# The last head group's chain set out anew, the first tile's turning and up products ahead of the last value products, three chunks' weights among the expert tiles

## Chip, core and metric

One core of one Trainium2 chip runs the whole program. The metric is the device time of one execution in microseconds (us).

## The reference

One transformer block over 2048 tokens of 128 channels, float32:

```
mod = silu(c) @ wmod                      # shift, scale and gate for two halves
h   = layernorm(x) * (1 + ca) + sa
x   = x + ga * (softmax(q k^T / sqrt(8) + alibi, causal) v @ W_proj + b_proj)   # 16 heads of 8
h   = layernorm(x) * (1 + cb) + sb
p   = softmax(h @ router_w^T)             # 8 experts, the best two per token
w   = softmax(of the two best p)
x   = x + gb * sum over the two of w * scale[e] * (silu(h @ w1[e]^T) @ w2[e]^T)
```

The experts are 512 wide. A token's two experts depend on the data.

## The kernel before, in words

**Attention.** The 16 heads go in four groups of four. Tokens are in four chunks of 512 columns. A first pass finds row maxima (scores on TensorE, maxima on VectorE, which the profile calls DVE), a second makes scores anew, exponentials on ScalarE (ACT; `probs`, L1295) and value products on TensorE (L744). A group has 36 steps of the second pass (`STEPS`); each step has two half-steps of two heads, and `step(p)` (L787) issues scores of step p, then the value products of step p-1. Step 36 (`NSTEP`) has the last value products alone. Chunk 3 begins at step 21. On every engine the order is written out by hand: tables at the top (L148 to L185) say at which step, or at which expert tile, an operation is issued.

**The last group's chain.** In the fourth group the first pass is through early, and the steps carry the second half of the block for chunks 0 to 2: `project(c)` on TensorE (`PROJECT`, L157, half of it behind each half-step), `residual(c)` with the statistics on DVE (L1032), `deviation(c)` on GpSimd (POOL; L1340, at step `DEVIATION_AT` and, for chunk 2, behind the group), `scale_tokens(c)` on DVE (L911; it normalises four tiles of 128 tokens into `slots`), `turn_late(c)` on TensorE (L650, `TURN`), `features(c, 1)` on ScalarE (L1215), `logits(c)` on TensorE (L656, `LOGITS`), `keep_logits` and `route(c, 0..5)` on DVE (L1041, L1046), two small exponentials on ScalarE (`route_exp`, L1252, `ROUTE_EXP`: step and position among the step's exps), `count(k)` on TensorE (L666, `COUNT`) and `place(k, 0..2)` on DVE (L1090). Part 5 of `route` makes the two weights of a token; only the join at the end reads them. POOL meanwhile also scales earlier values by their sums (`scale_values`, L1421, two multiplies or adds of 128x512; chunk 2 at step 20, chunk 3 at step 21).

**The experts.** Tokens are sorted by expert in three parts: part 0 is chunk 0, part 1 chunks 1 and 2, part 2 chunk 3. `send_part(k)` (L1451) has POOL write each token row twice into `slot_scratch` by an indirect DMA of 128 rows, with a memset (`pause`) ahead of each: 8 sends for part 0, 16 for part 1, 8 for part 2. Within part 1, `SEND_BREAK` says after how many sends POOL makes the deviation of chunk 3. There are 53 tiles of 128 rows: 15, 23 and 15. The SP queue loads a tile (L562; a part's first load waits for all of its sends) and stores results (L567). For tile j TensorE turns the rows (`turn_tile`, L837, one tile ahead), ScalarE makes features (L1316), TensorE the up products (`up`, L844), ScalarE silu (L1322), TensorE the down products of the tile before (`down`, L861). DVE copies each tile's first weights into a ring of four (`stage`, L1131, three tiles ahead) and multiplies the result by the gate (`keep`, L1143). Chunk 3's own chain runs among the tiles by `LATE_PROJECT` and the other LATE tables (L179 to L182). `gather_part(k)` (L1462) has POOL fetch each token's two results when all tiles of the part are stored; `join` (L1151) on DVE adds them with the weights.

**Between the two.** Behind step 36 TensorE waits for chunk 2's features, its logits and part 0's places, turns tiles 0 and 1 and starts the up products. ScalarE copies the last values (`copy_values`, L1262) and then makes tile 0's features. DVE, in its list at L1157, makes the weights of chunks 0 to 2 behind the placing of part 1, then scales by the sums of chunk 3 (`scale_sums`, `add_sums`, L970) and enters the tile loop, where it stages tile 3 first.

## Time and profile before

| | |
|---|---|
| median of three runs | 585.2 us (584.65 to 585.96) |
| the profiled execution | 584.42 us, of which the span between first and last instruction is 582.6 |
| TensorE, matmul (PE) and weight load (PEld) | 495.7 us (85%) and 266.1 (46%) |
| DVE | 456.4 us (78%) |
| ScalarE (ACT) | 403.3 us (69%) |
| POOL | 176.2 us (30%) |
| mean granted TensorE clock | 0.955 |

The page cuts the span into 40 slices of 14.6 us; each digit is a busy share in tenths, and PEclk the clock that TensorE was granted, in tenths of its full 2.4 GHz.

```profile
PE   4756777889999999999999998998988997999960
DVE  3689999989989998988998998986688744653442
ACT  4922456669878888888888888787788464555520
POOL 3410000010022120410214001057075681870884
PEclk9975899999999999999999999999899997999995
```

Setup takes the first four slices, attention goes on to about 448 us, the expert tiles to about 563, and the last slice is POOL's last gathers and the joins. All times in texts and rows are microseconds from the start of the span.

### The profile page before, as it was taken

How to read it: one execution, taken by the hardware profiler on the slowest of the kernel's cores; microseconds unless marked ns; L12 is line 12 of the kernel's file. 1: busy time of each engine (PE TensorE's matmuls, PEld its weight loads, DVE VectorE, ACT ScalarE, POOL GpSimd, SP SyncE). 2: the span in 40 equal slices, each digit the busy share in tenths (PEclk: the TensorE clock that was granted, in tenths of full speed). 3: DMA queues.
4: the chain of work that ended last, by engine and by line, in shares of the span. 5: the costliest groups of instructions: out<-in, count | busy, mean ns of one | idle time of the engine just before them, and what ended most of it. 6: DMA issues, size and time to landing. Idle time of an engine off the chain costs nothing.

```text
span 582.6 us, 15494 instructions
## 1 busy us (share of the span) xinstructions
PE 495.7 (85%) x5876; PEld 266.1 (46%) x5876; DVE 456.4 (78%) x775; ACT 403.3 (69%) x778; POOL 176.2 (30%) x291
## 2 busy tenths in 40 slices
PE   4756777889999999999999998998988997999960
PEld 2422233343243343243343333334434987999960
DVE  3689999989989998988998998986688744653442
ACT  4922456669878888888888888787788464555520
POOL 3410000010022120410214001057075681870884
PEclk9975899999999999999999999999899997999995
DMA  6593121000012530222300000100221212333332
GB/s 156 198 292 74 30 56 29 1 3 4 11 29 60 169 131 2 92 74 44 78 10 4 2 2 4 30 9 6 88 78 57 78 60 75 104 102 92 106 87 72
DMA packets 38263, 37.86 MB, mean 65 GB/s; under 512 B 7088, under 2 KB 33904, under 8 KB 37560
## 3 DMA queue, kind: packets, MB, share of 16 engines
q1 hardware_dynamic: 35808, 32.26, 20.0%
q0 software_dynamic: 2048, 4.20, 2.4%
q8 instruction: 49, 0.80, 0.6%
q10 hardware_dynamic: 336, 0.42, 0.2%
q14 instruction: 22, 0.18, 0.1%
HBM read 20.05 MB, written 16.61 MB: 63 GB/s over the span
## 4 chain that ended last, share of the span: by engine, by line
PE 51%; ACT 8%; POOL 8%; DVE 6%; issue 4%; DMA 1%; ACTq 0%; POOLq 0%; DVEq 0%
PE pv L744 18%; PE b L777 13%; ACT probs L1295 6%; PE b L716 6%; PE b L851 4%; PE b L868 4%; POOL raw L1470 4%; DVE part L1012 3%; PE b L691 3%; POOL pause L1442 2%; POOL slot_scratch L1449 1%; ACT raw L1265 1%; PE b L646 1%; PE b L842 1%; PE b L663 1%
## 5 line engine op out<-in xcount | busy, mean ns | idle before, releaser
L1295 ACT ACTIVATE probs<-b 128x512 f32<-128x512 f32 (+1 forms) x576 | 298.6, 571 | 77.2 <-PE b L691 34.3
L1012 DVE TENSOR_REDUCE part<-b 128x2 f32<-128x1024 f32 (+2 forms) x320 | 327.4, 1060 | 25.2 <-PE b L691 11.7
L744 PE MATMUL pv<-probs,v_cur 128*32 128x256 f32 (+1 forms) x2432 | 175.3, 370 | 0.3 <-ACT probs L1295 0.2
L777 PE MATMUL b<-aug 55*128 55x512 bf16 (+3 forms) x640 | 113.2, 352 | 24.8 <-ACT probs L1295 20.6
L716 PE MATMUL b<-aug 52*128 52x512 bf16 (+3 forms) x640 | 115.8, 361 | 20.1 <-DVE part L1012 17.2
L777 PEld LDWEIGHTS b<-aug 55*128 55x128 bf16 x640 | 36.9, 93 | 135.7 <-ACT probs L1295 129.8
L744 PEld LDWEIGHTS pv<-probs,v_cur 128*32 128x32 f32 x2432 | 49.9, 108 | 66.5 <-issue 38.9
L851 PE MATMUL b<-hTt,inverse 128*128 128x128 f32 x424 | 58.1, 281 | 1.3 <-ACT hTt L1316 1.1
L868 PE MATMUL b<-w2T_sb,hst 128*128 x424 | 57.1, 279 | 1.2 <-ACT hst L1322 0.8
L851 PEld LDWEIGHTS b<-hTt,inverse 128*128 128x128 f32 x424 | 53.2, 197 | 1.9 <-issue 1.3
L868 PEld LDWEIGHTS b<-w2T_sb,hst 128*128 128x128 f32 x424 | 52.5, 195 | 1.8 <-issue 1.6
L716 PEld LDWEIGHTS b<-aug 52*128 52x128 bf16 x640 | 33.5, 94 | 36.3 <-DVE part L1012 29.0
L1322 ACT ACTIVATE hst<-b 128x512 f32<-128x512 f32 x53 | 31.6, 597 | 23.0 <-PE b L851 21.6
L1141 DVE COPY inverse<-aug 128x512 f32 x53 | 26.2, 496 | 22.8 <-issue 19.7
L1413 POOL CAST nmp<-nmax 128x16 bf16<-128x16 f32 x16 | 3.4, 211 | 131.5 <-POOLq L191 131.3
L1442 POOL MEMSET pause<- 128x512 f32 x56 | 31.8, 567 | 33.7 <-DMA y_scratch<-aug 27.2
L1316 ACT ACTIVATE hTt<-b,modc 128x128 f32<-128x128 f32 x53 | 24.1, 456 | 25.6 <-PE b L842 16.3
L1149 DVE TENSOR_TENSOR aug<-b,gate 128x128 f32<-128x128 f32 x53 | 15.3, 290 | 30.7 <-issue 19.2
L1449 POOL DMA_INDIRECT slot_scratch<-slots,spots x32 | 32.8, 1024 | 8.9 <-POOL pause L1442 8.9
L1470 POOL DMA_INDIRECT raw<-y_scratch,spots x32 | 31.8, 993 | 9.0 <-POOL pause L1442 6.5
L691 PE MATMUL b<-maskQ,identh 64*128 64x128 bf16 (+1 forms) x512 | 32.4, 209 | 0.0
L691 PEld LDWEIGHTS b<-maskQ,identh 64*128 64x128 bf16 x512 | 25.6, 98 | 12.3 <-issue 1.8
(150 smaller groups left out, 379.0 us busy)
## 6 DMA issues: line engine op xcount, KB each, us to landing
xt<-slot_scratch SPq DMA_DIRECT2D x53, 64.0 KB, 1.9
y_scratch<-aug SPq DMA_DIRECT2D x53, 64.0 KB
slot_scratch<-slots SPq DMA_DIRECT2D x3, 1024.0 KB, 8.6
aug<-q_scratch SPq DMA_DIRECT2D x6, 384.0 KB
aug<-k_scratch SPq DMA_DIRECT2D x6, 384.0 KB
w2T_sb<-in_w2T SPq DMA_DIRECT2D x1, 2048.0 KB, 7.6
aug<-in_w1T SPq DMA_DIRECT2D x8, 256.0 KB
q_scratch<-pieces SPq DMA_DIRECT2D x4, 384.0 KB, 2.8
```

Of the source, the lines that this page charges most:

```text
L691: ins = mm(pair[half][:, at_ + c0:at_ + c1], identh[k, h, :], table[k, h, c0:c1], start=False, stop=True, skip_group_check=True)
L716: ins = mm(pair[half][:, at_:at_ + w], q_aug[buf][n, b, t:t + P], k_aug[buf][n, b, c * CW:c * CW + w], start=True, stop=True)
L744: return mm(pv[32 * hh:32 * hh + 32, c0:c1], v_cur[:, kb, hh, :], probs[:, step_ % 2, hh, at_:at_ + c1 - c0], start=(kb == 0 and c0 == 0), ...
L777: done.append(mm(pair[half][:, at_:at_ + w], k_aug[g % 2][n, b, kb * P:kb * P + P], q_aug[g % 2][n, b, (j + 1) * CW - w:(j + 1) * CW], sta ...
L851: last = mm(b1[:, j % 2, f * P:(f + 1) * P], w1s[:, k, f * P:(f + 1) * P], hTt[:, j % 2, :], start=True, stop=True)
L868: last = mm(b1[:, 2 + j % 2, 0:C], hst[:, j % 2, f, :], w2T[:, ds(e * FC + f, 1), :], start=(f == 0), stop=(f == FC - 1))
L1012: ins = nc.vector.tensor_reduce(dst, b1[:, slot:slot + 2, at_:at_ + w], AX.X, ALU.max)
L1295: nc.scalar.activation(probs[:, p % 2, hh, 0:w], b2[:, (n2 - 1) % RING2, 0:w], ACT.Exp).then_inc(exp_done, 1)
L1322: nc.scalar.activation(hst[:, j % 2, :, :].rearrange("p f t -> p (f t)"), b1[:, j % 2, :], ACT.Silu).then_inc(silu_s, 1)
L1442: own.inc(nc.gpsimd.memset(pause[:, :], 0.0))
L1449: nc.gpsimd.indirect_dma_start(slot_dram, bass.IndirectOffsetOnAxis(ap=spots[:, b, n:n + 1], axis=0), slots[:, n, :], None).then_inc(sent_ ...
L1470: nc.gpsimd.indirect_dma_start(yfin[:, n, b, :], None, y_dram[0:BASE[k + 1] * P, :], bass.IndirectOffsetOnAxis(ap=spots[:, b, n:n + 1], ax ...
```

## The change

The chain of chunks 1 and 2 in the last group is moved one to three steps forward; the tile tables of chunk 3 move two tiles back; the break in part 1's sends moves from 8 sends to 12. DVE scales chunk 2's tokens before the last piece of part 0's placing. TensorE turns tile 0 (into another bank, `turned_rows`) and makes its up products before the last value products. ScalarE makes tile 0's features and silu and tile 1's features before it copies the last values. The weights of chunks 0 to 2 go to tiles 22, 24 and 26. `turn_tile` and `up` are moved up in the file unchanged but for the bank.

```diff
 STACK_AT = {True: [START[1], START[1] + 2, START[1] + 4, START[1] + 6], False: [0, 5, 7, 11]}
 LAST_OUT, LAST_IN, LAST_INVERT, LAST_BACK, LAST_INVERSE = [5, 11], [6, 12], [INVERT, 14], [9, 15], [10, 16]
 LAST_SCALE = {13: 0, 18: 1}
-DEVIATION_AT = {19: 0, 22: 1}
-PROJECT = {16: 0, 19: 1, 24: 2}
-TURN = {19: 0, 22: 1, 28: 2}
-LOGITS = {21: 0, 23: 1, 29: 2}
-ROUTE_EXP = {(22, 4): (0, 0), (24, 4): (1, 0), (27, 4): (0, 1), (30, 2): (2, 0), (31, 4): (1, 1), (35, 4): (2, 1)}
-COUNT = {25: 0, 33: 1}
+DEVIATION_AT = {19: 0, 20: 1}
+PROJECT = {16: 0, 18: 1, 24: 2}
+TURN = {19: 0, 20: 1, 27: 2}
+LOGITS = {21: 0, 22: 1, 28: 2}
+ROUTE_EXP = {(21, 4): (0, 0), (24, 2): (1, 0), (26, 2): (0, 1), (29, 2): (2, 0), (30, 4): (1, 1), (34, 2): (2, 1)}
+COUNT = {25: 0, 32: 1}
 
 
 PARTS = [(0, TPC), (TPC, 3 * TPC), (3 * TPC, NT)]
@@ -176,13 +176,14 @@
 STORE_BEHIND = 6
 
 
-LATE_PROJECT, LATE_RESIDUAL, LATE_TOKENS, LATE_TURN, LATE_LOGITS, LATE_KEEP = 3, 4, 6, 7, 9, 10
-LATE_ROUTE = {10: 0, 12: 1, 13: 2, 14: 3, 15: 4, 21: 5}
-LATE_EXP = {11: 0, 16: 1}
-LATE_COUNT, LATE_PLACE = 16, {17: 0, 18: 1, 19: 2}
+LATE_PROJECT, LATE_RESIDUAL, LATE_TOKENS, LATE_TURN, LATE_LOGITS, LATE_KEEP = 3, 4, 8, 9, 11, 12
+LATE_ROUTE = {12: 0, 14: 1, 15: 2, 16: 3, 17: 4, 23: 5}
+LATE_EXP = {13: 0, 18: 1}
+LATE_COUNT, LATE_PLACE = 18, {19: 0, 20: 1, 21: 2}
+WEIGHTS_AT = {22: 0, 24: 1, 26: 2}
 JOIN_AT = {27: 0, 28: 1, 29: 2, 30: 3, 44: 4, 46: 5, 48: 6, 50: 7, 52: 8}
 STORE_AT = {36: 0}
-SEND_BREAK = 8
+SEND_BREAK = 12
 
 
 def take(e, s, n):
@@ -425,6 +426,10 @@
 
             return raw[:, g % 2, j * CW:(j + 1) * CW]
 
+
+        def turned_rows(j):
+
+            return b2[:, j % 2, 0:P] if j else b1[:, 1, 0:P]
 
         def last_part(q):
 
@@ -676,6 +681,23 @@
                               start=False, stop=(i == n_b - 1), skip_group_check=True)
                 last.then_inc(count_ps, 1)
 
+            def turn_tile(j):
+                k = j % ROWS_DEEP
+                pe.wait_ge(xt_in[k], 16 * (j // ROWS_DEEP + 1))
+                if j >= 2:
+                    pe.wait_ge(tT_s, j - 1)
+                nc.tensor.transpose(turned_rows(j), xt[:, k, :], ident[:, :]).then_inc(tT_ps, 1)
+
+            def up(j):
+                k = j % DEEP
+                pe.wait_ge(w1s_s, j + 1)
+                pe.wait_ge(tT_s, j + 1)
+                if j >= 2:
+                    pe.wait_ge(silu_s, j - 1)
+                for f in range(FC):
+                    last = mm(b1[:, j % 2, f * P:(f + 1) * P], w1s[:, k, f * P:(f + 1) * P], hTt[:, j % 2, :], start=True, stop=True)
+                last.then_inc(up_ps, 1)
+
             freed = []
             n_exp = [0]
 
@@ -820,6 +842,9 @@
                         if p in COUNT:
                             count(COUNT[p])
                     if last and p == NSTEP:
+                        pe.wait_ge(hT_s, 2 * NC_ - 1)
+                        turn_tile(0)
+                        up(0)
                         for b in range(PAIRS):
                             value_products(p, b)
 
@@ -833,23 +858,6 @@
             group(2, False, False)
             group(3, False, True)
 
-
-            def turn_tile(j):
-                k = j % ROWS_DEEP
-                pe.wait_ge(xt_in[k], 16 * (j // ROWS_DEEP + 1))
-                if j >= 2:
-                    pe.wait_ge(tT_s, j - 1)
-                nc.tensor.transpose(b2[:, j % 2, 0:P], xt[:, k, :], ident[:, :]).then_inc(tT_ps, 1)
-
-            def up(j):
-                k = j % DEEP
-                pe.wait_ge(w1s_s, j + 1)
-                pe.wait_ge(tT_s, j + 1)
-                if j >= 2:
-                    pe.wait_ge(silu_s, j - 1)
-                for f in range(FC):
-                    last = mm(b1[:, j % 2, f * P:(f + 1) * P], w1s[:, k, f * P:(f + 1) * P], hTt[:, j % 2, :], start=True, stop=True)
-                last.then_inc(up_ps, 1)
 
             def owner_of(j):
 
@@ -868,15 +876,12 @@
                     last = mm(b1[:, 2 + j % 2, 0:C], hst[:, j % 2, f, :], w2T[:, ds(e * FC + f, 1), :], start=(f == 0), stop=(f == FC - 1))
                 last.then_inc(down_ps, 1)
 
-            pe.wait_ge(hT_s, 2 * NC_ - 1)
             pe.wait_ge(lraw_s, NC_ - 1)
-            pe.wait_ge(place_s, 1)
-            turn_tile(0)
             for j in range(TILES):
                 if j + 1 < TILES:
                     turn_tile(j + 1)
-                up(j)
                 if j:
+                    up(j)
                     down(j - 1, owner_)
                 owner_ = owner_of(j)
                 if j == LATE_PROJECT:
@@ -1167,8 +1172,10 @@
             for k in range(1, 5):
                 route(0, k)
             residual(2)
-            place_part(0)
+            place(0, 0)
+            place(0, 1)
             scale_tokens(2)
+            place(0, 2)
             for k in range(1, 5):
                 route(1, k)
             keep_logits(2)
@@ -1178,8 +1185,6 @@
             for k in range(1, 5):
                 route(2, k)
             place_part(1)
-            for c in range(3):
-                route(c, 5)
             scale_sums(NC_ - 1)
             add_sums(NC_ - 1)
             for j in range(TILES):
@@ -1197,6 +1202,8 @@
                     route(NC_ - 1, LATE_ROUTE[j])
                 if j in LATE_PLACE:
                     place(NPART - 1, LATE_PLACE[j])
+                if j in WEIGHTS_AT:
+                    route(WEIGHTS_AT[j], 5)
                 if j in JOIN_AT:
                     join(JOIN_AT[j])
             keep(TILES - 1)
@@ -1300,8 +1307,6 @@
                         features(TURN[p], 1)
                     if last and (p, HG) in ROUTE_EXP:
                         route_exp(*ROUTE_EXP[p, HG])
-                if last:
-                    copy_values(g, NC_ - 1)
                 return n2
 
             n2 = group(0, True, False, 0)
@@ -1313,7 +1318,7 @@
                 act.wait_ge(tT_ps, j + 1)
                 if j >= 2:
                     act.wait_ge(up_ps, j - 1)
-                nc.scalar.activation(hTt[:, j % 2, :], b2[:, j % 2, 0:P], ACT.Identity, bias=modc[:, 2:3], scale=modc[:, 3:4]).then_inc(tT_s, 1)
+                nc.scalar.activation(hTt[:, j % 2, :], turned_rows(j), ACT.Identity, bias=modc[:, 2:3], scale=modc[:, 3:4]).then_inc(tT_s, 1)
 
             def silu(j):
                 act.wait_ge(up_ps, j + 1)
@@ -1322,7 +1327,10 @@
                 nc.scalar.activation(hst[:, j % 2, :, :].rearrange("p f t -> p (f t)"), b1[:, j % 2, :], ACT.Silu).then_inc(silu_s, 1)
 
             tile_features(0)
-            for j in range(TILES):
+            silu(0)
+            tile_features(1)
+            copy_values(G - 1, NC_ - 1)
+            for j in range(1, TILES):
                 if j + 1 < TILES:
                     tile_features(j + 1)
                 silu(j)
```

## Rows read from the trace of the kernel before

**Rows 1.** The chain that ended last, two steps: start us, us, engine, line.

```profile
535.69 1.60 DMA y_scratch<-aug
...
576.12 2.48 DMA raw<-y_scratch,spots
```

**Rows 2.** Timeline of POOL, 446 to 481: start us, us, engine, line, op.

```profile
446.09 0.52 POOL L1442 MEMSET pause<- 128x512 f32 x1 [4.87 <-DVE spots L1116]
...
463.55 0.23 POOL L1345 TENSOR_SCALAR rstd<-mv 128x4 f32<-128x4 f32 x1 [2.72 <-DVE mv L908]
...
465.14 0.65 POOL L1442 MEMSET pause<- 128x512 f32 x1
...
479.71 0.97 POOL L1449 DMA_INDIRECT slot_scratch<-slots,spots  x1 [0.28 <-POOL pause L1442]
```

**Rows 3.** Timeline of TensorE in the tiles, 455 to 491.

```profile
455.47 1.16 PE L851 MATMUL b<-hTt,inverse 128*128 128x128 f32 x8 [0.28 <-DVE inverse L1141]
...
458.36 1.06 PE L851 MATMUL b<-hTt,inverse 128*128 128x128 f32 x8
...
464.05 1.06 PE L851 MATMUL b<-hTt,inverse 128*128 128x128 f32 x8
...
467.16 1.06 PE L851 MATMUL b<-hTt,inverse 128*128 128x128 f32 x8
...
471.80 1.06 PE L851 MATMUL b<-hTt,inverse 128*128 128x128 f32 x8
...
479.33 1.15 PE L868 MATMUL b<-w2T_sb,hst 128*128 x8 [0.79 <-ACT hst L1322]
...
483.74 0.48 PE L842 MATMUL b<-ident_sb,xt 128*128 128x128 f32 x1 [3.25 <-DMA xt<-slot_scratch]
...
490.33 1.06 PE L851 MATMUL b<-hTt,inverse 128*128 128x128 f32 x8
```

**Rows 4.** Three stretches: busy us by engine (x count), granted clock, DMA, GB/s.

```profile
410.00:415.00 5.00, 4.75 (x38) 1.63 (x34) 2.82 (x5) 3.85 (x9) 0.00 (x0) 0.66 0.34 105
...
480.00:492.00 12.00, 8.75 (x55) 8.56 (x54) 4.27 (x13) 3.16 (x7) 0.68 (x1) 0.72 0.26 72
...
498.00:510.00 12.00, 12.00 (x110) 12.00 (x110) 8.60 (x32) 6.50 (x13) 10.07 (x15) 1.00 0.37 106
```

**Rows 5.** Timelines of POOL, DVE and TensorE, steps 18 to 21.

```profile
398.35 1.27 POOL L1427 TENSOR_TENSOR raw<-raw,inverse 128x512 f32<-128x512 f32 x1
...
398.41 2.63 DVE L917 TENSOR_SCALAR slots<-x_sb,mv,rstd 128x128 f32<-128x128 f32 x2 [1.48 <-POOL rstd L1354]
...
403.81 0.69 DVE L1037 TENSOR_TENSOR x_sb<-b,x_sb 128x512 f32<-128x512 f32 x1 [0.19 <-PE b L646]
...
406.51 0.39 PE L777 MATMUL b<-aug 55*128 55x512 bf16 x2
...
407.30 1.11 DVE L917 TENSOR_SCALAR slots<-x_sb,mv,rstd 128x128 f32<-128x128 f32 x4 [1.48 <-POOL rstd L1354]
```

**Rows 6.** Timelines of ScalarE and DVE where attention ends, 446 to 452.

```profile
446.70 0.66 ACT L1295 ACTIVATE probs<-b 128x256 f32<-128x256 f32 x2 [0.28 <-PE b L691]
...
449.71 1.28 ACT L1322 ACT_TABLE_LOAD   x1
...
451.00 0.60 ACT L1322 ACTIVATE hst<-b 128x512 f32<-128x512 f32 x1
...
451.10 0.70 DVE L974 STREAM_TRANSPOSE q<-raw 128x512 f32<-128x512 f32 x1
```

**Rows 7.** Timelines of TensorE, the SP queue and DVE, 439 to 449.

```profile
439.07 0.64 PE L744 MATMUL pv<-probs,v_cur 128*32 128x256 f32 x8
...
442.21 0.20 PE L672 MATMUL b<-both,lowerb 128*128 128x64 bf16 x1
...
442.51 6.24 SPq L562 DMA_DIRECT2D xt<-slot_scratch  x7
...
445.85 0.16 DVE L1082 TENSOR_SCALAR psm<-wtop 128x4 f32<-128x4 f32 x1
```

## The prediction

> **What bounds the kernel now.** I read the chain of waits from its end first. It leaves TensorE for the last time with the store of tile 37 at 535.69, and from there POOL's row gathers hold it until the last lands at 578.6 [rows 1]. Those gathers start when tile 37 is stored and their number doesn't change, so the time at which TensorE is through tile 37 sets the end: a microsecond won by tile 16 is won at the end, if nothing between waits anew.
>
> What TensorE waits for before tile 37 is part 1. On POOL, its first send follows the placing at 446.09, eight sends take until 460.83, then POOL stands 2.72 us for the variances of chunk 3, spends 1.59 on the deviation, and the other eight end at 480.68 [rows 2]. On TensorE, tile 14 turns tile 15's rows first; that turning waits 3.25 us, until 483.74 [rows 3]. The windows show the second price: the granted clock averages 0.72 from 480 to 492, which at the two levels of 1.2 and 2.4 GHz is 6.7 us at the lower one [rows 4]. From 483.74 to the up products of tile 16 at 490.33 two tiles took 6.6 us; two tiles at the upper level take 3.8 (458.36 to 464.05 is three) [rows 3].
>
> **From tile 3 to tile 16.** TensorE needs without any wait for part 1: tile 3 to 4 with the late projection 2.89; tiles 4 to 9 at 1.90 each 9.5 (the turning has left tile 7); tile 9 to 10 with the turning and a wait like the one measured 3.11; tile 10 to 11 1.9; 11 to 12 with the logits 4.64 less 1.90, 2.74; 12 to 16 four times 1.9, 7.6; and the exponential at tile 13, whose table loads cost the down products 0.79 when they stood at tile 11 (tile 15's wait hid that), 0.8. Sum 28.5; it was 490.33 less 455.47, 34.9 [rows 3]. **Gain 6.4**, if POOL is in time. The part that is the clock, 2.7, is gained only if TensorE doesn't stand still for long there.
>
> **What the moved steps cost in the last group.** Projection and deviation of chunk 1 go three POOL and DVE steps forward, and there a collision stands. Before, DVE's first two scalings of chunk 0 ran beside POOL's multiplies of 1.27 us and took 2.63 together; the same instructions with POOL idle took 1.11 for four [rows 5]. So a scaling next to such a multiply is as long as the multiply. In the new order deviation 1 stands between POOL's two pairs of multiplies. Chunk 0's scaling then meets one pair only and ends at 398.41 + 2.63 + 0.6 = 401.6; the residual, the statistics and the deviation of chunk 1 take 407.30 less 403.81, 3.49, so its scaling starts at 405.1; but now POOL's second pair starts with it, and it ends at 405.1 + 2.63 + 0.6 = 408.3 instead of 408.4 [rows 5]. Nearly nothing is won for chunk 1, while TensorE is sent to turn it at the end of step 20, which ended at 406.51 [rows 5]. With the projections moved within the same steps this arrival hardly shifts: TensorE waits 1.8 us, with all scores behind it, ScalarE's exps wait for the scores, and the turning (with the features behind it on ScalarE) now stands there too. I take **2.2 lost**; the ends are 0 (the scaling isn't stretched) and 2.5. The early logits and exps then feed DVE sooner, but DVE's route of chunk 0 still waits for what comes after this stall.
>
> The clock was at the lower level for 3.4 us of the stretch 410 to 415, although TensorE was busy for 4.75 of 5 us there [rows 4]. After a stall the engine has less behind it, so I let this stretch recur at its present cost, which is in the time before. Tiles at the lower level took 6.6 for 3.8, 0.7 lost per microsecond of full-speed work; 3.4 us hold 2.0 of such work, so 1.4, and as ScalarE sets part of the pace in attention I take 1.0 as the present cost. If the stretch doesn't recur, that comes back; if it lasts like the other, 6.7 us, 1.7 more is lost. The shift of the last exp is thus **+2.2, from 1.2 to 3.9**, and from -1.0 if there is no stall.
>
> **The turn into the tiles.** The last exp ended at 447.36 (446.70 + 0.66), the table load began at 449.71, silu at 451.00, DVE's scaling by the sums at 451.10, the up products of tile 3 at 455.47, 8.1 after the last exp [rows 3, 6]. Up product 0 now goes ahead of the last value products: ScalarE makes the features, loads the table under the up products, silu is done about 2.5 after the last exp. But the value products wait in line behind the up products, and the copy behind silu and the second features, so the copy ends about 3.7 after the last exp (an estimate: up products 1.16, load 1.28, silu 0.60, a copy as long as silu). DVE, which until then made three chunks' weights and is free now, starts its scaling there, at 3.8, against 3.74 before; tile 3 is 4.37 behind it in both. **Gain 0**, ends -0.4 and +0.4: what the weights free on DVE, the later copy takes back.
>
> ScalarE's switch was 1.28 long, and silu began 0.01 behind its end [rows 6]; so the sum takes nothing beyond the load. The Trainium skill (ScalarE: Activation LUTs, What ACT_TABLE_LOAD costs) adds a drain of about 1.38 us to each switch; as the copy now stands behind it, that would put tile 3 some 1.4 later and the gain at 2.8. The measured pair shows no drain of that size, and the sum goes by the pair.
>
> **POOL.** Chunk 2's count stood at 442.21, and the first send 3.88 behind it [rows 2, 7]. It moves to the end of step 32, 439.7 (439.07 + 0.64), plus the shift of 2.2: 441.9, first send 445.8. Twelve sends at 1.84 are 22.1, the deviation 1.6 (its wait is gone: the variances stood at 463.5, with the shift 465.7), four at 1.94 7.8: last send ends 477.3; as before, 3.06 from there to tile 15's turning: 480.4. TensorE is there at 447.36 + 2.2 + 8.1 + 23.9 = 481.6. POOL is in time by 1.2, so TensorE sets the pace. Deviation 3 is ready at 469.5; DVE wants it behind tile 7's result, about 470. The waits for chunk 2's features and tile 0's rows now stand ahead of the last value products. Part 0 is placed behind chunk 2's scaling, at most 2.5 later; SP's first tile loads stood from 442.51 [rows 7], so the first is issued by 445.0, and TensorE comes at 449: no cost; with the cover gone, each microsecond of lateness holds the last value products as long.
>
> **Weights among the tiles.** Three times 1.75 (445.85 to 451.10) [rows 6, 7] go behind the stage at tiles 22, 24, 26. From 498 to 510, with chunk 3's placing and weights among the tiles, DVE was busy for 8.60 of 12 us and TensorE for all 12 [rows 4]: 3.4 free, 5.25 wanted, so DVE falls about 1.9 behind and makes it up over the tiles after. Down products wait for the result two tiles back, which leaves two tiles less the half tile of the products, 2.85: the lag hides, cost 0. Cover gone, each weight costs up to 1.75, the three 5.25.
>
> **Sum.** 6.4 + 0 - 2.2 = 4.2. Against the profiled execution's 584.42: 580.2. The median of three, 585.2, is 0.8 above it; on that base **581.0**.
>
> **The rivals.** *No stall at step 20* (0.15): rstd is early enough that DVE slips in between, or POOL's multiplies come first. For it: the ready time without stretch is 406.2, just in time. Against: the stretched row is the same pair of lines. Shift -1.0 to 0, gain 6.4 to 7.4: 578.3.
> *POOL still sets tile 15* (0.15): sends more than 1.2 later than worked out, by a later count or slower sends; each microsecond beyond costs one, and a wait like the measured one brings the low clock back: gain 1 to 2.5, about 583.5.
> *DVE falls behind in tiles 19 to 30* (0.10): the lag passes 2.85 and TensorE waits for results or staged weights; 1.5 to 2 of the gain, about 582.8.
> *A dearer switch* (0.03): ScalarE is held in front of the copy for one more load's length, 1.28, and DVE's scaling and tile 3 with it: gain 2.9, 582.3. Against: the pair above. (The Trainium skill's drain, above, would be of this kind.)
> *Slower* (0.06): the clock stays low from the stall at step 20 through the rest of attention. Place: steps 21 to 36, 406.5 to 447.4. At half of the tiles' 0.7 per microsecond (ScalarE sets part of the pace) it decides once it costs 5.4, the 4.2 and the 1.2 that can be told, which is after some 15 us of such work; through all 40.9 it costs 14: 585.2 - 4.2 + 14 = 595. Against: the low stretch there ended after 3.4 us.
> *The change does nothing* (0.04): the earlier steps are all eaten, 585.
> The forecast itself has 0.47 with its own range from shift and turn, 579.6 to 583.1.
>
> **Numbers.** The range 578.0 to 584.0 takes in most of the first and second rivals and leaves out the slower ones and the best of the first. About 0.2% (1.2 us) can be told from no change here: faster 0.85 (forecast, no stall, switch, most of POOL and DVE), same 0.09, slower 0.06.
>
> **What would show it.** Right: scaling of chunk 1 again near 3.2 us and TensorE idle some 2 us before its turning; no wait of POOL at the deviation; tile 15's turning without a DMA wait and no low clock after it; tile 3 some 8.1 behind the last exp; DVE's results late by up to 2 in tiles 22 to 30 with TensorE still at 1.90 a tile; the gathers' length unchanged. Wrong: a wait on tile 15 again, a tile pace above 1.90 in 20 to 30, a last exp earlier than 447.4 or later than 451.3.

## The result, and the profile after

The changed kernel took 591.37 us (591.21 to 592.77, 4 runs), the kernel before 585.58 (584.65 to 586.39, 4 runs) on the same chip: ratio 1.0108, 95% interval 1.0093 to 1.0124. It is **slower by 1.1%**; 581.0 had been predicted.

Both profiles are cut at the same five events, which makes a table of differences (us; the events are TensorE's first projection of chunk 0 in step 16, the end of the last exp, the start of the up products of tile 3 and of tile 16, the end of the span):

| stage | before | after | after less before | predicted |
|---|---|---|---|---|
| start to the projection | 392.64 | 395.43 | +2.79 | 0 |
| projection to last exp | 54.72 | 59.90 | +5.18 | +2.2 |
| last exp to tile 3 | 8.11 | 7.66 | -0.45 | 0 |
| tile 3 to tile 16 | 34.86 | 29.47 | -5.39 | -6.4 |
| tile 16 to the end | 92.27 | 96.89 | +4.62 | 0 |
| span | 582.6 | 589.4 | +6.8 | -4.2 |

What the change was made for has come, 5.4 us of it. It is lost again, and more, in the last head group and behind tile 16, and the start came later too. The rows, in that order. First the chain that ended last, as in [rows 1] (start, us, engine, what):

```profile
542.40 1.60 DMA y_scratch<-aug
...
582.87 2.47 DMA raw<-y_scratch,spots
```

Tile 37 is stored 6.7 us later than in [rows 1], and the gathers behind it are as long as they were: the end follows tile 37, as argued.

**The gain.** POOL's timeline shows that the wait for chunk 3's variances, 2.72 in [rows 2], is gone: no bracket stands behind the deviation any more, and the pause memsets and sends run on until 482.97.

```profile
474.02 0.26 POOL L1353 TENSOR_SCALAR rstd<-mv 128x4 f32<-128x4 f32 x1
```

TensorE's timeline up to tile 16 has no wait for xt, where [rows 3] has 3.25 us, and the granted clock stays at the upper level:

```profile
478.29 0.66 PE L605 MATMUL b<-ident_sb,slots 128*128 128x128 f32 x4 [0.98 <-DVE slots L922]
...
489.22 1.06 PE L698 MATMUL b<-hTt,inverse 128*128 128x128 f32 x8
491.06 1.15 PE L876 MATMUL b<-w2T_sb,hst 128*128 x8 [0.79 <-ACT hst L1327]
...
492.46 0.78 PE L698 MATMUL b<-hTt,inverse 128*128 128x128 f32 x5
```

**The last group.** At the end of step 20 TensorE stands 1.91 us for chunk 1's scaled tokens (1.8 had been worked out). Timelines of DVE, POOL and TensorE:

```profile
401.21 3.16 DVE L922 TENSOR_SCALAR slots<-x_sb,mv,rstd 128x128 f32<-128x128 f32 x4 [1.48 <-POOL rstd L1362]
...
407.77 3.14 DVE L922 TENSOR_SCALAR slots<-x_sb,mv,rstd 128x128 f32<-128x128 f32 x4 [1.48 <-POOL rstd L1362]
```

```profile
406.38 0.23 POOL L1353 TENSOR_SCALAR rstd<-mv 128x4 f32<-128x4 f32 x1 [2.61 <-DVE mv L913]
...
407.71 1.27 POOL L1435 TENSOR_TENSOR raw<-raw,inverse 128x512 f32<-128x512 f32 x1
```

```profile
408.41 0.64 PE L766 MATMUL pv<-probs,v_cur 128*32 128x128 f32 x16
410.97 0.66 PE L605 MATMUL b<-ident_sb,slots 128*128 128x128 f32 x4 [1.91 <-DVE slots L922]
...
412.09 1.08 PE L766 MATMUL pv<-probs,v_cur 128*32 128x128 f32 x16
```

The value products behind it take 1.08 us where the same form took 0.64 in front of it: the lower clock. In the kernel before it lasted 3.4 us here [rows 4]. Now the windows (length, busy us of PE, PEld, DVE, ACT, POOL, granted clock, DMA share, GB/s) show it for 13.6 us, 411.6 to 425.2, with TensorE busy for all but 0.02 us of the last two windows:

```profile
406.00:413.00 7.00, 4.73 (x70) 2.53 (x62) 3.43 (x8) 4.17 (x10) 3.78 (x4) 0.90 0.12 37
413.00:420.00 7.00, 6.98 (x41) 3.89 (x37) 3.60 (x8) 4.16 (x9) 0.00 (x0) 0.50 0.15 46
420.00:427.00 7.00, 7.00 (x49) 2.48 (x49) 4.45 (x19) 4.15 (x9) 0.00 (x0) 0.63 0.21 69
```

**The turn.** Between the last exp and the table load ScalarE makes nothing but tile 0's features; DVE waits 7.91 us for the values' copy, which now stands behind silu and the next features:

```profile
454.67 0.66 ACT L1302 ACTIVATE probs<-b 128x256 f32<-128x256 f32 x2 [0.28 <-PE b L713]
...
455.98 1.28 ACT L1327 ACT_TABLE_LOAD   x1
457.28 0.60 ACT L1327 ACTIVATE hst<-b 128x512 f32<-128x512 f32 x1
...
458.59 0.59 ACT L1272 ACTIVATE raw<-pv 128x512 f32<-128x512 f32 x1
```

```profile
459.21 0.71 DVE L979 STREAM_TRANSPOSE q<-raw 128x512 f32<-128x512 f32 x1 [7.91 <-ACT raw L1272]
```

**The weights among the tiles.** From 510 to 522 TensorE is busy for 9.79 of 12 us. DVE's kept rows (L1154) come 2.76, 3.36 and 3.72 us apart with one chunk's weights between each two, while TensorE at its own pace does a tile in 1.90. The weights in the middle are chunk 3's own: `LATE_ROUTE` has them at tile 23, between the moved ones of tiles 22 and 24:

```profile
509.01 0.29 DVE L1154 TENSOR_TENSOR aug<-b,gate 128x128 f32<-128x128 f32 x1
509.78 0.43 DVE L1146 COPY inverse<-aug 128x512 f32 x1 [0.48 <-issue]
510.12 0.16 DVE L1087 TENSOR_SCALAR psm<-wtop 128x4 f32<-128x4 f32 x1
...
511.77 0.29 DVE L1154 TENSOR_TENSOR aug<-b,gate 128x128 f32<-128x128 f32 x1
...
513.04 0.57 DVE L1087 TENSOR_SCALAR psm<-wtop 128x4 f32<-128x4 f32 x1
...
515.13 0.29 DVE L1154 TENSOR_TENSOR aug<-b,gate 128x128 f32<-128x128 f32 x1
515.97 0.86 DVE L1146 COPY inverse<-aug 128x512 f32 x1 [0.55 <-issue]
516.75 0.57 DVE L1087 TENSOR_SCALAR psm<-wtop 128x4 f32<-128x4 f32 x1
...
518.85 0.29 DVE L1154 TENSOR_TENSOR aug<-b,gate 128x128 f32<-128x128 f32 x1
```

```profile
499.24 0.19 PE L677 MATMUL b<-both,lowerb 128*128 128x32 bf16 x1 [0.97 <-DVE both L1080]
...
515.68 1.15 PE L876 MATMUL b<-w2T_sb,hst 128*128 x8 [0.78 <-ACT hst L1327]
...
519.39 1.15 PE L876 MATMUL b<-w2T_sb,hst 128*128 x8 [1.18 <-DVE aug L1154]
```

The silu that the down products at 515.68 need, and two of POOL's memsets:

```profile
513.01 0.60 ACT L1327 ACTIVATE hst<-b 128x512 f32<-128x512 f32 x1 [0.43 <-PE b L698]
```

```profile
512.90 0.68 POOL L1450 MEMSET pause<- 128x512 f32 x1
...
516.61 0.68 POOL L1450 MEMSET pause<- 128x512 f32 x1
```

```profile
510.00:522.00 12.00, 9.79 (x81) 9.10 (x80) 9.57 (x40) 4.71 (x10) 10.27 (x13) 1.00 0.29 84
```

The wait at 515.68 is put down to ScalarE, but the silu that these down products need had ended at 513.61 (the row of 513.01). They also need the result buffer that DVE's keep at 515.13 to 515.42 clears, and they start 0.26 behind it.

### The profile page after: what moved, and what is told of

Its sections match the earlier page's. It is cut to its first block, busy times and chain, and to the rows that moved or that the text cites. A ratio compares the mean times of both kernels' runs of the same rounds, so it can differ in the third digit from the quotient of the medians.

```text
span 589.4 us, 15495 instructions
## 1 busy us (share of the span) xinstructions
PE 502.4 (85%) x5876; PEld 266.7 (45%) x5876; DVE 457.7 (78%) x775; ACT 403.7 (68%) x778; POOL 176.1 (30%) x291
## 4 chain that ended last, share of the span: by engine, by line
PE 51%; ACT 8%; DVE 8%; POOL 6%; issue 4%; DMA 1%; DVEq 0%; ACTq 0%; POOLq 0%
PE pv L766 18%; PE b L799 13%; PE b L738 6%; ACT probs L1302 6%; PE b L876 4%; PE b L698 4%; POOL raw L1478 4%; DVE part L1017 3%; PE b L713 3%; POOL pause L1450 1%; DVE slots L922 1%; ACT raw L1272 1%; PE b L668 1%; PE b L689 1%; DVE inverse L1146 1%
## 5 line engine op out<-in xcount | busy, mean ns | idle before, releaser
L766 PE MATMUL pv<-probs,v_cur 128*32 128x256 f32 (+1 forms) x2432 | 178.4, 375 | 0.2
L799 PE MATMUL b<-aug 55*128 55x512 bf16 (+3 forms) x640 | 115.3, 359 | 24.0 <-ACT probs L1302 19.2
L738 PE MATMUL b<-aug 52*128 52x512 bf16 (+3 forms) x640 | 117.4, 367 | 19.1 <-DVE part L1017 16.0
L698 PE MATMUL b<-hTt,inverse 128*128 128x128 f32 x424 | 56.7, 277 | 0.8 <-ACT hTt L1321 0.6
L698 PEld LDWEIGHTS b<-hTt,inverse 128*128 128x128 f32 x424 | 51.5, 192 | 1.3 <-issue 1.0
L1146 DVE COPY inverse<-aug 128x512 f32 x53 | 26.3, 496 | 22.5 <-issue 20.0
L1154 DVE TENSOR_TENSOR aug<-b,gate 128x128 f32<-128x128 f32 x53 | 15.4, 291 | 23.1 <-PE b L876 12.5
```

What stands on the lines that cost most here:

```text
L698: last = mm(b1[:, j % 2, f * P:(f + 1) * P], w1s[:, k, f * P:(f + 1) * P], hTt[:, j % 2, :], start=True, stop=True)
L738: ins = mm(pair[half][:, at_:at_ + w], q_aug[buf][n, b, t:t + P], k_aug[buf][n, b, c * CW:c * CW + w], start=True, stop=True)
L766: return mm(pv[32 * hh:32 * hh + 32, c0:c1], v_cur[:, kb, hh, :], probs[:, step_ % 2, hh, at_:at_ + c1 - c0], start=(kb == 0 and c0 == 0), ...
L799: done.append(mm(pair[half][:, at_:at_ + w], k_aug[g % 2][n, b, kb * P:kb * P + P], q_aug[g % 2][n, b, (j + 1) * CW - w:(j + 1) * CW], sta ...
L1146: V.tensor_copy(w1s[:, j % DEEP, :], w1T[:, ds(e * F, F)]).then_inc(w1s_s, 1)
```

## The experiments

**Theory** after the result: the stall at step 20 sets off the long stretch at the lower clock, and the weights among the tiles hold up the kept rows. **Rivals**: the earlier chain's work is dear by itself; the weights hide, and the loss behind tile 16 is the later count; the late start belongs to the change. A table gathers what each run's profile gave in the stages of the first table, with the length of the low-clock stretch in the last group (from the granted clock in windows of half a microsecond). The letters stand for the parts: C = chunk 1's chain as in the change, L = late steps two tiles later and the break of the sends at 12, W = weights among the tiles, T = turn and up ahead.

| run | parts | start to projection | to last exp | low clock | to tile 3 | to tile 16 | to the end |
|---|---|---|---|---|---|---|---|
| before | - | 392.64 | 54.72 | 3.4 | 8.11 | 34.86 | 92.3 |
| before_same | - | 393.51 | 54.89 | 3.4 | 8.12 | 34.75 | 92.3 |
| before_same2 | - | 393.72 | 53.84 | 0 | 8.12 | 33.96 | 92.7 |
| after | C L W T | 395.43 | 59.90 | 13.6 | 7.66 | 29.47 | 96.9 |
| after_same | C L W T | 394.76 | 62.29 | 20.5 | 7.64 | 29.48 | 96.8 |
| weights_back | C L T | 395.24 | 62.27 | 20.5 | 7.64 | 29.48 | 93.4 |
| chunk1_back | L W T | 394.79 | 55.08 | 0 | 8.28 | 29.43 | 96.8 |
| scale_early | C L W T, multiplies early | 394.82 | 56.22 | 6.8 | 7.67 | 29.47 | 96.8 |
| combo | L T | 396.77 | 56.32 | 3.4 | 8.29 | 29.45 | 93.4 |
| before_chunk1_early | C | 395.78 | 60.41 | 13.6 | 7.63 | 33.45 | 92.7 |
| before_late | L | 396.63 | 53.85 | 0 | 8.11 | 29.41 | 93.4 |
| before_break | break alone | 394.30 | 53.83 | 0 | 8.11 | 34.50 | 92.7 |
| chunk1_turn21 | C, turning at 21 | 394.48 | 56.34 | 6.8 | 7.62 | 34.53 | 92.2 |
| stall19 | a stall alone | 395.64 | 57.02 | 3.4 | 7.61 | 31.71 | 92.8 |
| weights_spread | L T, weights at 22, 34, 38 | 393.18 | 55.97 | 3.4 | 8.29 | 29.44 | 94.7 |

### The change again, and each suspect undone

after_same is the changed kernel unchanged.

> The changed kernel again, unchanged, for its profile alone. In the first one it came to the projection of chunk 0 in the last group 2.8 us later than the kernel before, because the clock was at its lower level until 70 and not until 63 at the start. If that is chance, this profile may come there 0 to 3 us earlier; if it belongs to the changed program, it comes there again within 0.3 us, at 395.4.

weights_back puts the three chunks' weights back ahead of the last sums:

```diff
-WEIGHTS_AT = {22: 0, 24: 1, 26: 2}
+WEIGHTS_AT = {}
...
+            for c in range(3):
+                route(c, 5)
             scale_sums(NC_ - 1)
```

> The changed kernel with the three weight computations back in front of the scaling by the last sums. Theory: DVE's lag at tiles 18 to 26 costs 2.5 to 3.5 us there, while in front of the tiles DVE now stands idle for 7.9 us, so the 5.25 us of weights fit: 2.5 to 3.5 us faster than the changed kernel, some 588, and tile 24 to 26 at 1.90 each. Rival: the lag is chunk 3's own chain (count, places), and the weights only sit on it: under 1 us faster.

chunk1_back takes chunk 1's chain back to its steps:

```diff
-DEVIATION_AT = {19: 0, 20: 1}
-PROJECT = {16: 0, 18: 1, 24: 2}
-TURN = {19: 0, 20: 1, 27: 2}
-LOGITS = {21: 0, 22: 1, 28: 2}
-ROUTE_EXP = {(21, 4): (0, 0), (24, 2): (1, 0), (26, 2): (0, 1), (29, 2): (2, 0), (30, 4): (1, 1), (34, 2): (2, 1)}
+DEVIATION_AT = {19: 0, 22: 1}
+PROJECT = {16: 0, 19: 1, 24: 2}
+TURN = {19: 0, 22: 1, 27: 2}
+LOGITS = {21: 0, 23: 1, 28: 2}
+ROUTE_EXP = {(22, 4): (0, 0), (24, 4): (1, 0), (26, 2): (0, 1), (29, 2): (2, 0), (30, 4): (1, 1), (34, 2): (2, 1)}
```

> The changed kernel with chunk 1's deviation, projection, turning and logits back at their old steps, the rest as changed. Theory (the stall and its low clock come from chunk 1's turning at step 20): no wait of 1.9 at the turning, the low stretch shrinks from 13 us to 4 or less, and the last exp comes 4 to 5.5 us earlier than in the changed kernel; 586 or so. Rival (the clock falls there anyway, by the products of steps 20 to 24): the low stretch stays 10 us or more and only 2 us come back.

scale_early has POOL's multiplies for chunks 2 and 3 out of the way of the scalings:

```diff
-SCALE_AT = [13, 14, 20, 21]
+SCALE_AT = [13, 14, 14, 14]
```

> The changed kernel with POOL's multiplies for chunks 2 and 3 moved from steps 20 and 21 to step 14, where POOL stood idle; nothing else. Theory (DVE's scaling is held up by those multiplies): chunk 0's and chunk 1's scaling take 1.1 us each and not 3.2, TensorE's wait at the turning goes from 1.9 to 0.3 or less, and with it most of the low stretch; 4 to 5.5 us faster than the changed kernel, about 586. Rival (DVE's chain is too long for step 20 by itself): the wait stays above 1 us, under 2 us faster.

Measured: after_same 592.86 (one run); weights_back 589.47, ratio to before 1.0062 (1.0045 to 1.0078); chunk1_back 586.21, 1.0013 (1.0001 to 1.0026); scale_early 587.3, 1.0035 (1.0015 to 1.0055). In the table weights_back differs from after_same by nothing but the last column: 3.4 us. Its window from 510 to 522 has TensorE busy throughout:

```profile
510.00:522.00 12.00, 12.00 (x110) 12.00 (x110) 8.47 (x31) 6.55 (x14) 9.87 (x13) 1.00 0.42 117
```

chunk1_back has neither the stall nor a low-clock stretch, and its last exp comes 4.8 us sooner behind the projection. So both terms are shown, and their places. In scale_early the scalings of chunks 0 and 1 take 1.12 and 1.11 us and the wait at the turning is gone, as expected; 6.8 us of low clock are left all the same, and 587.3 is more than the 586 expected. What is left in weights_back's last column, 1.1 over before, is lost between the up products of tiles 16 and 22 (13.75 us there, 12.72 in before); the largest single wait is that at the later count (0.97 at 499.24 above).

combo has both undone.

> The kernel after, with chunk 1's chain at its old steps and the three chunks' weights back in front of the last sums. If the two losses add (low-clock stretch of the last group gone: 5 us; weights out of the tiles: 3.5 us from tile 16 to the end, as the two single undoings showed): chunk1_back's 586.2 less 3.5 = 582.7 us, ratio 0.995, and no wait on VectorE's aug around tile 28. Rival: with the last exp 8 us earlier the three weights (three times about 1.1 us of VectorE) no longer lie in an idle stretch in front of the last sums, tile 3 of the MLP waits 3 us more for inverse, and the time is 585.5 to 586 us.

584.32 us against 586.30, ratio 0.997 (0.9957 to 0.9983): faster than before, by less than expected. The last column falls to 93.4 as in weights_back. Tile 3 does not wait longer than in chunk1_back (8.29 and 8.28), so the rival is out; but 8.28 is worse than before's 8.11, of which more below.

### One part alone, put into the kernel before

before_chunk1_early has C only.

```diff
-DEVIATION_AT = {19: 0, 22: 1}
-PROJECT = {16: 0, 19: 1, 24: 2}
-TURN = {19: 0, 22: 1, 28: 2}
-LOGITS = {21: 0, 23: 1, 29: 2}
-ROUTE_EXP = {(22, 4): (0, 0), (24, 4): (1, 0), (27, 4): (0, 1), (30, 2): (2, 0), (31, 4): (1, 1), (35, 4): (2, 1)}
+DEVIATION_AT = {19: 0, 20: 1}
+PROJECT = {16: 0, 18: 1, 24: 2}
+TURN = {19: 0, 20: 1, 28: 2}
+LOGITS = {21: 0, 22: 1, 29: 2}
+ROUTE_EXP = {(21, 4): (0, 0), (24, 2): (1, 0), (27, 4): (0, 1), (30, 2): (2, 0), (31, 4): (1, 1), (35, 4): (2, 1)}
```

> The kernel before, with chunk 1's chain alone moved (deviation 22 to 20, projection 19 to 18, turning 22 to 20, logits 23 to 22, exps two steps earlier). Theory (the stall at step 20's turning sets off the long low-clock stretch): TensorE waits 1.8 to 2 us there, then runs at the lower clock for 10 to 17 us, the last exp ends at 451.5 to 454 in place of 447.4, and the time is 589 to 591 us, ratio 1.007 to 1.010. Rival 1 (the low stretch needs the tighter order of the whole change, chunk 2 a step earlier too): stall of 1.9 us, low stretch 3 to 4 us, 586 to 587 us. Rival 2 (the loss came from elsewhere): 585 to 586 us.

590.76 us, ratio 1.0078 (1.0055 to 1.0102). This one part, with nothing else of the change, loses 0.8%. Its four executions aren't alike: 591.78 (the profiled one) and 592.62 us at a mean granted clock of 0.940 and 0.941, 589.73 and 589.70 at 0.949 and 0.952. Its stall, and its windows:

```profile
411.31 0.66 PE L600 MATMUL b<-ident_sb,slots 128*128 128x128 f32 x4 [1.90 <-DVE slots L917]
```

```profile
413.00:420.00 7.00, 6.57 (x35) 3.60 (x36) 3.60 (x8) 4.50 (x10) 0.00 (x0) 0.50 0.14 40
420.00:427.00 7.00, 7.00 (x44) 2.78 (x48) 4.46 (x19) 3.37 (x7) 0.00 (x0) 0.53 0.24 75
```

before_late has L only.

```diff
-LATE_PROJECT, LATE_RESIDUAL, LATE_TOKENS, LATE_TURN, LATE_LOGITS, LATE_KEEP = 3, 4, 6, 7, 9, 10
-LATE_ROUTE = {10: 0, 12: 1, 13: 2, 14: 3, 15: 4, 21: 5}
-LATE_EXP = {11: 0, 16: 1}
-LATE_COUNT, LATE_PLACE = 16, {17: 0, 18: 1, 19: 2}
+LATE_PROJECT, LATE_RESIDUAL, LATE_TOKENS, LATE_TURN, LATE_LOGITS, LATE_KEEP = 3, 4, 8, 9, 11, 12
+LATE_ROUTE = {12: 0, 14: 1, 15: 2, 16: 3, 17: 4, 23: 5}
+LATE_EXP = {13: 0, 18: 1}
+LATE_COUNT, LATE_PLACE = 18, {19: 0, 20: 1, 21: 2}
...
-SEND_BREAK = 8
+SEND_BREAK = 12
```

> The kernel before, with the last chunk's late steps two tiles later and the break of the sends at 12 in place of 8, and nothing else. Theory (GpSimd's sends in time for tile 15 are the whole gain of the tile stretch): no wait of 3.25 us for xt at tile 15 and no low clock behind it, tile 3 to tile 16 in 29.0 to 29.9 us in place of 34.9, about 1 us of it given back by VectorE being late at the last chunk's count, so 580.5 to 581.5 us, ratio 0.992 to 0.994. Rival (GpSimd comes in time only because the turn and up are ahead and the values' copy is behind them): the wait at tile 15 stays at 1.5 to 3 us and the time is 583.5 to 585.5 us.

582.16 us against 586.30, ratio 0.9926 (0.9909 to 0.9943): the whole gain, from this part alone. POOL is in time only just, with a wait of 0.44 us left at the place of the 3.25:

```profile
483.39 0.33 PE L842 MATMUL b<-ident_sb,xt 128*128 128x128 f32 x1 [0.44 <-DMA xt<-slot_scratch]
```

before_break has the break of the sends alone (`SEND_BREAK = 12`).

> The kernel before with the break of GpSimd's sends at 12 in place of 8 and nothing else. Theory (break and shift need each other: with the break alone, GpSimd comes to the last chunk's deviation some four sends later, and the turning at tile 7 waits for it): no wait at tile 15, but TensorE waits 3 to 5 us for the last chunk's slots around tile 7, where before waited 0.56, with a low clock behind it: 584 to 587 us. Rival (the break alone is the gain, the two tiles are not needed): no wait of over 1 us at tile 7 and 581.5 to 582.5 us, ratio 0.993.

586.39 us, ratio 1.0033 (1.0014 to 1.0052). The stall has moved from tile 15 to tile 7, as the theory had it:

```profile
471.48 0.90 PE L600 MATMUL b<-ident_sb,slots 128*128 128x128 f32 x3 [4.71 <-DVE slots L917]
```

So the break and the two tiles belong together.

### Is it the stall or the chain?

Two runs separate them. chunk1_turn21 is before_chunk1_early with `TURN = {19: 0, 21: 1, 28: 2}`, the chain without the stall. stall19 is the kernel before with a stall and nothing moved; VectorE writes chunk 0's scaled tokens twice more before they count:

```diff
             if c == 0:
                 dve.wait_ge(blank_out, BLANKS)
+                for n in [*range(TPC)] * 2:
+                    own.inc(nc.vector.tensor_scalar(slots[:, n, :], x_sb[:, n, :], mv[:, n, 0:1], rstd[:, n:n + 1], ALU.subtract, ALU.mult))
+                    if n == TPC - 1:
+                        own.wait()
```

> before_chunk1_early with TensorE's turning of chunk 1 a step later (21 in place of 20), its other steps as there. Theory (the stall of 1.9 us at step 20 sets off the long low-clock stretch, and nothing else in the earlier chain does): no wait of over 0.6 us there, low clock for at most 4 us as in before, the last exp within 1 us of before's 54.7 us after the projection of step 16, 585 to 587 us. Rival (the earlier chain itself, by its denser work on VectorE and TensorE, is what is dear): the low-clock stretch of 10 us and more comes without the stall, 589 to 591 us.

> The kernel before, with chunk 0's scaling on VectorE run three times over (the same values written again, eight scalings more), so that the turning of chunk 0 at step 19 finds its tokens late; nothing of the chain's order is changed. Theory (a stall of TensorE of about 2 us among steps 19 to 21 sets off the long stretch at the lower clock, whatever the order): TensorE waits 2 to 4 us at step 19's turning, then 7 to 17 us at the lower clock, the last exp ends 58.5 to 62 us after step 16's projection where before shows 54.7, 589 to 592 us. Rival (it is the earlier chain's content that is dear, not the stall): the wait itself and the 3 to 4 us at the lower clock that before has too, 56.5 to 58 us after the projection, 587 to 588 us.

chunk1_turn21: 583.58 us (582.19 to 587.21, 10 runs) against 585.27, ratio 0.998 (0.996 to 1.0001). Its profiled execution took 587.06; in it TensorE stands only 0.30 us before the turning, yet runs for 6.8 us at the lower clock. It is not typical of the ten: five took 582.19 to 582.79 at a mean granted clock of 0.959, the profiled one had 0.943. stall19: 588.12 against 586.08, ratio 1.004 (1.0019 to 1.0061). Its stall is as long as the change's, and behind it the low clock lasts 3.4 us, as in before:

```profile
409.01 0.66 PE L600 MATMUL b<-ident_sb,slots 128*128 128x128 f32 x4 [2.23 <-DVE slots L921]
```

```profile
413.00:420.00 7.00, 6.05 (x62) 2.85 (x58) 4.07 (x10) 6.54 (x13) 0.00 (x0) 0.90 0.34 104
```

The theory falls in its simple form: a stall by itself costs its own 2.2 us (57.02 against 54.8) and no more. The 20 profiles, taken together: stall and earlier chain, 13.6 or 20.5 us of low clock (4 profiles); the earlier chain without the stall, 6.8 (scale_early, chunk1_turn21 and late_turn21 below) or none (late_turn21_scale and after_repaired below); the stall without the chain, 3.4 (stall19, one profile, though none of its ten executions took over 589.33); neither of the two, 3.4 or none (10 profiles). So the long stretch was seen with both together and with neither alone. Which work of the chain does it stays open: no run took the turning, the logits or the exps out one at a time.

### The weights, the count, the turn ahead

weights_spread is chunk1_back with `WEIGHTS_AT = {22: 0, 34: 1, 38: 2}`.

> chunk1_back with the weights of the three chunks at tiles 22, 34 and 38 in place of 22, 24 and 26. From tile 16's up products to the end chunk1_back has 96.8 us, combo (weights in front of the tiles) 93.4. Theory (VectorE has no spare time from tile 16 on, so each weights step ahead of tile 37's store pushes the kept rows back by its own length, some 1.15 us): two of the three lie ahead of that store, 95.7 us. Rival (only the crowd of the three right behind the count and the places is dear; a single one is caught up within some tiles): 93.4 to 94.2 us.

94.7 us from tile 16 to the end, between the two expectations, with 93.4 for no weights there and 96.8 for three: the one at tile 22, among the last chunk's placing, costs 1.4 (tile 28 starts 26.57 us behind tile 16, in combo 25.14), and the one at tile 34 nothing: the distance stays the same from there to the last tile. From 522 to 534 TensorE is busy for 12.00 of 12 us in this run.

before_late_count19 is before_late with the count moved on (and chunk 3's own weights from tile 23 to 24), late_count19_ahead adds the turn ahead (with the change's order of places and copy).

```diff
-LATE_COUNT, LATE_PLACE = 18, {19: 0, 20: 1, 21: 2}
+LATE_COUNT, LATE_PLACE = 19, {20: 0, 21: 1, 22: 2}
```

> before_late (late steps two tiles later, break at 12) with the last chunk's count one tile later still (19, its places 20 to 22, its weights 24). Theory (the 0.97 us for which TensorE waits at tile 18's count, for VectorE's both, is a lag that one tile of 2.2 us covers): that wait falls under 0.2 us, tile 16 to the end 92.3 to 92.6 us in place of before_late's 93.4, 581 us, ratio to before 0.991. Rival (VectorE is behind for longer than a tile): the wait stays over 0.7 us and the time is before_late's, 582.2 us.

> before_late_count19 with the change's turn ahead: first tile's turn and up products in front of the last value products, the values' copy behind the first silu, the places in the change's order. Theory (what is ahead is worth at most the 0.45 us that after shows from the last exp to tile 3's up products, 7.66 in place of 8.11): 7.6 to 7.7 us there, and the time within 0.5 us of before_late_count19. Rival (VectorE's inverse for tile 3 comes later with the tables of before, as chunk1_back's wait of 0.73 us shows): 8.1 to 8.4 us there, no gain or 0.3 us lost. Rival 2 (it was worth more and hidden by what was late behind it): over 1 us faster than before_late_count19.

before_late_count19: 581.13 against 585.27, ratio 0.9926 (0.9907 to 0.9945), before_late's number. The wait at the count is gone, and two others have come in its place, 1.24 together; the last column stays at 93.4:

```profile
495.01 1.13 PE L851 MATMUL b<-hTt,inverse 128*128 128x128 f32 x8 [0.41 <-issue]
496.97 1.15 PE L868 MATMUL b<-w2T_sb,hst 128*128 x8 [0.83 <-ACT hst L1322]
```

late_count19_ahead: 582.17, ratio 0.9943 (0.9924 to 0.9962). Tile 3 comes 8.43 us after the last exp, later than without the turn ahead (8.13). Its first silu is early (450.95; 452.74 in before_late_count19), but the copy behind it ends at 452.99, and DVE, whose last weights instruction starts at 452.98, starts its scaling at 453.06, no earlier than in before_late_count19 (452.85):

```profile
452.40 0.59 ACT L1274 ACTIVATE raw<-pv 128x512 f32<-128x512 f32 x1
```

So the turn ahead gains nothing, and the 0.45 us that after shows are not its merit: before_chunk1_early and stall19, without it, have 7.63 and 7.61. DVE starts its scaling no earlier there, 3.75 us behind the last exp (3.74 in before, 3.88 in after). What differs is DVE's copy of tile 3's first weights, in before and in after:

```profile
454.43 0.99 DVE L1141 COPY inverse<-aug 128x512 f32 x1
```

```profile
462.51 0.43 DVE L1146 COPY inverse<-aug 128x512 f32 x1
```

It takes 0.43 us in the seven profiles with 7.6 or 7.7 us to tile 3, and 0.92 to 0.99 in the thirteen with 8.1 to 8.4. Why the copy is short in some stays open.

### Versions faster than both

late_turn21 is before_late_count19 with chunk1_turn21's tables, late_turn21_scale adds the early multiplies, after_repaired is the changed kernel with the losses taken out (turning at 21, multiplies early, weights in front, count at 19).

> before_late_count19 (late steps two tiles later, count three, break at 12) with chunk_1_turn21's early chain of chunk 1, turning at 21. Theory (the two gains lie in different stages and add): 585.3 times 0.9926 times 0.998, about 580 us, ratio 0.988 to 0.992, with no wait over 0.5 us at step 21 and a low-clock stretch that comes in some runs and not in others. Rival (chunk 1's chain at 21 gains nothing, its ten runs only fell well): ratio 0.992 to 0.995.

> late_turn21 with GpSimd's multiplies for chunks 2 and 3 at step 14, out of the way of VectorE's scalings at steps 18 to 20. Theory (these multiplies are what draws four scalings out to 3.1 us and more from 1.11): the scaling of chunk 0 takes 1.1 to 1.3 us, no wait at step 21's turning, at most 0.5 us faster than late_turn21. Rival (scale_early's times were no better for that: the early multiplies only move the collision into step 14): as late_turn21 within 0.5 us, or slower by up to 1.5 us.

> The kernel after with the two losses taken out and its order else kept: chunk 1's turning at step 21, GpSimd's multiplies for chunks 2 and 3 at step 14, the weights in front of the last sums, the last count at tile 19. From the stages of the other runs: projection at 395.2, last exp some 55 us later (53.8 in late_turn21_scale, 1.2 more for chunk 2 a step earlier, as chunk1_back against before_late), 7.7 us to tile 3, 29.4 to tile 16, 92.6 to the end, 1.8 around the span: 581.7 us, ratio 0.992 to 0.994. Rival (the step-20 logits and exps of the whole change, tighter than in late_turn21_scale, keep the clock low even without a wait): a stretch of 6 us or more at the lower clock, last exp 57 us or more after the projection, 583.5 to 586 us.

late_turn21: 582.36 us, ratio 0.9942 (0.9916 to 0.9968), with 6.8 us of low clock in its profile; that is the rival's range. late_turn21_scale: 580.99, 0.9918 (0.989 to 0.9947); after_repaired: 583.34, 0.9956 (0.9942 to 0.9971), slower than expected, without the rival's low clock. In late_turn21_scale the four scalings of a chunk take 1.11 us (chunk 0, at 401.29) and 1.12, and the last group has no low clock:

```profile
407.42 1.12 DVE L917 TENSOR_SCALAR slots<-x_sb,mv,rstd 128x128 f32<-128x128 f32 x4 [1.48 <-POOL rstd L1354]
```

```profile
413.00:420.00 7.00, 5.84 (x62) 2.77 (x62) 6.48 (x20) 5.51 (x12) 0.00 (x0) 1.00 0.32 96
```

The intervals of before_late, before_late_count19 and late_turn21_scale overlap: with the least edit, before_late, one has what can be shown, 0.7%. That the earlier chain adds anything to it is not shown, even with its stall gone. In after_repaired tile 3 stands at 8.26, not the 7.7 expected (its weight copy took 0.92), and the last column is 93.3, not 92.6.

before_same and before_same2 are the kernel before, unchanged.

> The kernel before, unchanged, for a second profile. If the late rise of the clock at the start (at about 70 us, where the one profile of before has 63.4) is chance: this profile may show it too, the projection of chunk 0 at step 16 lies anywhere from 392.6 to 395.5, and the time follows it. If it belongs to the changed program: the rise at 62 to 65 us again and the projection at 392.5 to 392.9.

> The kernel before, unchanged, a third profile. If the start is chance: the projection of chunk 0 anywhere from 392.6 to 396.8, and the span follows it. If a later start belongs to any edited program: 392.5 to 393.6 again.

They took 585.41 and 584.16 us, and their projection stands at 393.51 and 393.72. **The late start stays open.** Of 17 profiles of edited kernels one, weights_spread, starts as early (393.18), the others at 394.30 to 396.77, with a later rise of the clock, up to 73.1 us, a second fall at 74.9 to 77.4, or both; none of the edits touches what runs there. The three profiles of before speak against chance, weights_spread against a fixed cost of an edit. The executions that left no trace weaken the first: of the 87 of the kernel before that were timed beside these runs, 75 had a mean granted clock under 0.955, the lowest of the three profiles, so the unedited kernel too is at the lower clock for longer in most of its executions; in which stage can't be told without a trace. Of the change's 5.8 us, 1 to 2.8 may lie there, by the first column.

## Why the prediction was wrong

The span was forecast 4.2 us shorter and came out 6.75 longer. Of these 10.95 us, 4.6 lie behind tile 16, 3.0 in the last group, 2.8 in the start, 1.0 in the gain, and 0.45 came back at tile 3.

**What bounds the kernel, and the gain: right in mechanism, 1.0 too large.** Tile 37 sets the end, POOL's sends set tile 15, and with POOL in time the wait and the low clock behind it go (before_late). It was 5.4 for 6.4: the tile with the exponential cost 3.24 (489.22 to 492.46), 1.3 over the 1.90 of the others, where 0.8 was taken, and the tiles around the turning some 0.4 more. The margin of 1.2 us for POOL was thin: before_late still waits 0.44 there.

**The stall: right.** 1.8 to 2.2 predicted, 1.91 measured, by the collision of rows worked out from [rows 5]: a scaling beside a POOL multiply is as long as the multiply. late_turn21_scale shows it from the other side, with 1.11 for four. The Trainium skill (SBUF — State Buffer, SBUF: two separate sides) has VectorE and GpSimd exclude each other at a shared pair of ports for whole instructions; 3.14 against 1.12 agrees with that.

**The step that failed first: the length of the low-clock stretch.** The prediction let it "recur at its present cost", 3.4 us, and bounded it at 6.7 by the stretch behind tile 15. It was 13.6 and, in a second profile, 20.5. Its price was about right. For the slower rival 0.35 us was taken per microsecond of full-speed work, which is 0.26 per microsecond at the lower clock (0.35 over 1.35). The runs give 0.35 between the two profiles of the changed kernel (62.29 less 59.90, over 6.83), 0.34 in before_chunk1_early (60.41 less 53.85 less the stall of 1.90, over 13.6), and 0.21 in after against chunk1_back, which has the same order of chunk 2 (59.90 less 55.08 less 1.91, over 13.6). The slower rival had mechanism and place. By its own count it decides after some 15 us of such work, 20.8 us at the lower clock; the two profiles of the changed kernel lie below that and near it, and the weights' 3.4 us, which no rival added to it, came on top. It was given 0.06, on the ground that the stretch had ended after 3.4 us before. That was one profile, of another order of work. A length that had been seen once is no bound for a length under a new order.

**The second: "weights among the tiles, cost 0".** They cost 3.4. DVE's time that [rows 4] show as not busy, 3.4 of 12 us, was taken as free. Most of it isn't: ahead of most of the tiles' weight copies DVE stands some 0.47 us that the profile puts down to issue (the brackets above); the code has a register read of the tile's expert there. In the changed kernel this makes 20.0 us over 44 of the 53 copies (L1146, put down to issue).

Five of the six copies that begin in the 12 us of [rows 4] have such a bracket, 2.45 us together (three of the five are put down to TensorE's up products, at the same 0.46 to 0.58). With 0.95 free and 5.25 wanted the lag is 4.3, and 2.85 of cover leave 1.45, an estimate. The rest is argued from rows: DVE had chunk 3's own weights to make between the first two of the moved ones, and its own instructions lengthened there, the copy from 0.43 to 0.86, the first weight step from 0.16 to 0.57. Both long weight steps end 0.03 us behind one of POOL's `pause` memsets (513.61 and 513.58, 517.32 and 517.29, rows above); the short one at 510.12 has none beside it. The cover-gone price, 5.25 for the three, was more than the 3.4 measured; the tile 34 of weights_spread shows where a weight would have hidden.

**The turn: right at 0.** "What the weights free on DVE, the later copy takes back" is what chunk1_back shows (8.28 against 8.11). The 0.45 that after gained there came from the shorter weight copy, in a term that was taken as the same in both, 4.37 behind the scaling (3.78 in after); that was luck. ScalarE's switch was 1.28 again with silu 0.02 behind its end. The Trainium skill's drain of about 1.38 us beside each load (ScalarE: Activation LUTs, What ACT_TABLE_LOAD costs) isn't seen at 455.98 either.

**Not foreseen:** 1.1 us around the last count. With the wait for tile 15 gone, TensorE comes to the count 0.97 before `both` is ready, and moving the count only moves the wait. That in before this wait had let DVE catch up is argued, not shown. A wait that goes uncovers what had hidden behind it.

**The change's other parts.** Chunk 2 a step earlier costs 1.2 us in the last group: chunk1_back has 55.08 there and before_late 53.85, neither with a low clock. late_count19_ahead, which has the turn ahead and the change's order of places but chunk 2 at its old steps, has 53.84.
